# The second feed-forward of a two-layer gated decoder: all experts for all rows, or a dense shared expert and chosen rows in 39 blocks

## The reference, cut to what matters

```python
def _ffn(x, wg, wu, wd):
    return silu(x @ wg.T) * (x @ wu.T) @ wd.T       # 128 -> 344 -> 128
logits = xf @ gate_w.T                              # xf: 2048 x 128, 8 experts
topk_w, topk_idx = top_k(softmax(logits), 2)
topk_w = topk_w / (sum(topk_w) + 1e-20)
cw = zeros((T, 8)).at[arange(T)[:, None], topk_idx].set(topk_w)
y = sum over e of cw[:, e:e + 1] * _ffn(xf, wg[e], wu[e], wd[e])
y = y + _ffn(xf, swg, swu, swd)                     # shared expert
x = x + tanh(g_ffn[1]) * y
```

## Time and profile before

| | us |
|---|---|
| median of 3 runs | 796.5 (796.01 to 798.43) |
| the profiled execution | 796.5 |
| its span, first to last instruction | 794.8 |
| TensorE busy in the span | 658.4 |
| VectorE / ScalarE / GpSimd busy | 610.5 / 397.0 / 395.5 |

### The profile page before, as it was taken

The page is one execution under the profiler, slowest core; times in us unless marked ns, Lnnn a source line. Parts: engine busy times, 40 slices in busy tenths (PEclk is TensorE's granted clock), DMA queues, the critical chain, the costliest instruction groups (busy, mean ns, idle before and its releaser), DMA issues.

```text
span 794.8 us, 13507 instructions
## 1 busy us (share of the span) xinstructions
PE 658.4 (83%) x3446; PEld 499.5 (63%) x3446; DVE 610.5 (77%) x2037; ACT 397.0 (50%) x702; POOL 395.5 (50%) x399
## 2 busy tenths in 40 slices
PE   5653330188999999999999969998799999999995
PEld 2321110176787787877878846665678787877884
DVE  5799999687777777777777785688877777777774
ACT  5533110044565565555565644545456565565653
POOL 4047870036566666665666653000155666656663
PEclk9655555559999999999999975999799999999999
DMA  5424442205877677786776600000146765666761
GB/s 145 78 66 133 137 124 44 47 1 122 153 162 147 139 160 140 147 156 135 158 153 129 134 1 1 2 2 12 37 84 136 161 153 131 159 149 136 160 134 53
DMA packets 73810, 85.90 MB, mean 108 GB/s; under 512 B 39097, under 2 KB 51754, under 8 KB 70760
## 3 DMA queue, kind: packets, MB, share of 16 engines
q1 hardware_dynamic: 66714, 75.05, 44.7%
q0 software_dynamic: 4320, 9.68, 4.1%
q10 hardware_dynamic: 2734, 0.69, 0.4%
HBM read 76.69 MB, written 8.70 MB: 107 GB/s over the span
## 4 chain that ended last, share of the span: by engine, by line
PE 67%; DVE 23%; issue 5%; ACT 2%; DMA 2%; POOL 1%; DVEq 0%; SPq 0%; POOLq 0%; ACTq 0%
PE bank L1034 7%; PE bank L1035 7%; PE bank L1036 7%; PE bank_quad L1190 7%; PE bank_pair L1036 7%; PE bank_pair L1034 7%; PE bank_pair L1035 7%; PE bank_quad L1187 6%; PE bank_quad L1188 6%; DVE arena L1491 3%; PE bank_pair L1083 2%; DVE arena L1487 2%; PE bank L1126 2%; DVE arena L1445 2%; DVE arena L1435 2%
## 5 line engine op out<-in xcount | busy, mean ns | idle before, releaser
L695 POOL TENSOR_TENSOR act_lo<-arena,act_hi 128x512 fp32r<-128x512 f32 x232 | 300.5, 1295 | 193.6 <-ACT act_hi L868 190.8
L1724 DVE TENSOR_TENSOR bank_pair<-arena,bank_pair 128x512 f32<-128x512 f32 x220 | 152.5, 693 | 103.9 <-ACT arena L882 72.9
L882 ACT ACTIVATE arena<-bank 128x512 f32<-128x512 f32 x232 | 139.0, 599 | 185.6 <-PE bank L1036 185.6
L1732 DVE TENSOR_TENSOR arena<-bank_pair,arena 128x512 f32<-128x512 f32 x220 | 152.1, 691 | 16.7 <-DMA arena<-scr_mask 4.5
L868 ACT ACTIVATE act_hi<-arena 128x512 fp32r<-128x512 f32 x232 | 144.6, 623 | 12.8 <-DVE arena L1722 7.1
L1034 PE MATMUL bank_pair<-xn_hi,w_hi 128*128 128x512 f32 x232 | 92.6, 399 | 2.9 <-DVE arena L1722 2.1
L1190 PE MATMUL bank_quad<-act_lo,w_hi 128*128 128x512 f32 x232 | 92.5, 399 | 3.0 <-POOL act_lo L695 3.0
L1034 PE MATMUL bank<-xn_hi,w_hi 128*128 128x512 f32 x232 | 93.8, 404 | 0.1
L1035 PE MATMUL bank<-xn_hi,w_lo 128*128 128x512 f32 x232 | 92.6, 399 | 0.0
L1036 PE MATMUL bank<-xn_lo,w_hi 128*128 128x512 f32 x232 | 92.5, 399 | 0.0
L1036 PE MATMUL bank_pair<-xn_lo,w_hi 128*128 128x512 f32 x232 | 92.3, 398 | 0.0
(11 more groups left out here) (220 smaller groups left out, 1072.6 us busy)
## 6 DMA issues: line engine op xcount, KB each, us to landing
arena<-scr_mask SPq DMA_DIRECT2D x94, 512.0 KB, 6.7
scr_w<-prep_out POOLq DMA_DIRECT2D x25, 192.0 KB, 2.2
w_raw<-scr_w SPq DMA_DIRECT2D x25, 192.0 KB, 6.3
w_raw<-in_L_ffn_expert_gate_k SPq DMA_DIRECT2D x32, 64.0 KB, 5.9
w_raw<-in_L_ffn_expert_up_k SPq DMA_DIRECT2D x32, 64.0 KB, 5.7
w_raw<-in_L_ffn_expert_down_k SPq DMA_DIRECT2D x64, 32.0 KB, 5.2
prep_in<-in_L_ffn_wg POOLq DMA_DIRECT2D x21, 64.0 KB, 2.3
prep_in<-in_L_ffn_wu POOLq DMA_DIRECT2D x21, 64.0 KB, 2.1
```

The lines of the kernel that those rows point to most:

```text
L695: nc.gpsimd.tensor_tensor(act_lo[:, k % 2, :], act_a[:, k % 2, :], act_hi[:, k % 2, :].bitcast(F32), ALU.subtract).then_inc(FF[f]["alo"], 1)
L882: nc.scalar.activation(act_s[:, k % 2, :], ps[4 + k % 2][:], ACT.Silu).then_inc(FF[f]["silu"], 1)
L1724: nc.vector.tensor_tensor(ps[6 + i][:], act_s[:, i, :], ps[6 + i][:], ALU.mult).then_inc(FF[f]["t"], 1)
L1732: nc.vector.tensor_tensor(act_a[:, i, :], ps[6 + i][:], mask[:, j, 512 * k:512 * (k + 1)], ALU.mult).then_inc(FF[f]["act"], 1)
```

## The change

The second feed-forward no longer computes all experts for all rows.

- **Preparation.** The weights are prepared in 27 groups (9 experts x 3 parts of up to 128 hidden numbers) and stored already split: ScalarE copies the high part, TensorE takes it off in PSUM with a matmul by minus one, ScalarE copies the low part; two stores for each group.
- **Dense part** (`dense`). The shared expert alone: 12 units of 9 matmuls. In between, VectorE runs the routing in three parts of 8, 4 and 4 tiles. It also counts, with triangular matmuls (`rows_ahead`), how many earlier rows chose the same expert, which gives each of the 4096 choices its row in a scratch memory with a region for each expert.
- **Send** (`send_rows`). GpSimd writes each tile's rows twice, once for each choice, with 32 indirect DMAs of 128 rows x 528 bytes; a row carries its number and its first expert. `block_table` on VectorE works out which expert and which first row each of 39 blocks of 128 rows has. SyncE then fills up each expert's last block with 8 stores at addresses from a register, and waits for them.
- **Block loop** (`sparse`), 39 blocks written out: SyncE reads a register and loads the block's rows (4 buffers); TensorE turns them, multiplies them by the expert's gate and up weights (which all lie on chip, addressed by a register), 344 columns at a time, turns the activation, and multiplies by the second projection; VectorE sums; GpSimd forms the target row numbers with three small instructions and writes the 128 results with an indirect DMA to a second scratch.
- **Combination** (`add_choices`). SyncE loads both choices' results in row order, VectorE adds them to x by their gate weights.

The core of the diff. SyncE:

```diff
+            sp.wait_ge(s_tab, 3)
+            sp.wait_ge(s_sent, 16 * 2 * TILES)
+            for e in range(E1):
+                n = sp.value_load(table[0:1, 2 * BLOCKS + e:2 * BLOCKS + e + 1], min_val=0, max_val=TOK)
+                sp.dma_start(scr_x[bass.ds(n + e * REGION, BLK), :], pad_rows[:, e, :]).then_inc(s_pad, 16)
+            sp.wait_ge(s_pad, 16 * (SPARE + E1))
+            for k in range(BLOCKS):
+                if k >= XBUF:
+                    sp.wait_ge(s_bt, k - XBUF + 1)
+                    sp.wait_ge(s_row, 3 * (k - XBUF + 1))
+                first = sp.value_load(table[0:1, k:k + 1], min_val=0, max_val=ROWS_X - BLK)
+                sp.dma_start(xb[:, k % XBUF, :], scr_x[bass.ds(first, BLK), :]).then_inc(s_x[k % XBUF], 16)
```

GpSimd:

```diff
+            def send_rows(part):
+
+                pool.wait_ge(s_pos, part + 1)
+                pool.wait_ge(s_xn, (3 * B + ROUTE_BATCH[part]) * ND)
+                pool.wait_ge(s_xnp, (3 * B + ROUTE_BATCH[part]) * (TPB - ND))
+                for t in range(TILES)[ROUTE_TILES[part]]:
+                    for c in range(2):
+                        pool.indirect_dma_start(out=scr_x, out_offset=bass.IndirectOffsetOnAxis(ap=row_of[:, t, c:c + 1], axis=0),
+                                                in_=xrow[:, t, :], in_offset=None).then_inc(s_sent, 16)
...
+            def block_rows_out(k):
+
+                i, j = k % XBUF, k % YBUF
+                pool.wait_ge(s_x[i], 16 * (k // XBUF + 2))
+                if k >= YBUF:
+                    pool.wait_ge(s_ys[j], 16 * (k // YBUF))
+                near, row = y_near[:, j:j + 1], y_row[:, j:j + 1]
+                nc.gpsimd.tensor_scalar(near, xb[:, i, COL_E:COL_E + 1], block_e[:, k:k + 1], float(-TOK),
+                                        ALU.is_equal, ALU.mult).then_inc(s_row, 1)
+                pool.wait_ge(s_row, 3 * k + 1)
+                nc.gpsimd.tensor_tensor(near, near, xb[:, i, COL_TOK:COL_TOK + 1], ALU.add).then_inc(s_row, 1)
+                pool.wait_ge(s_row, 3 * k + 2)
+                nc.gpsimd.tensor_copy(row, near).then_inc(s_row, 1)
+                pool.wait_ge(s_row, 3 * (k + 1))
+                pool.wait_ge(s_byc, k + 1)
+                pool.indirect_dma_start(out=scr_y, out_offset=bass.IndirectOffsetOnAxis(ap=row, axis=0),
+                                        in_=y_b[:, j, :], in_offset=None).then_inc(s_ys[j], 16)
...
+            dense_low(0)
+            normalise(3, B - 1)
+            for u in range(1, POOL_LO):
+                dense_low(u)
+            padding()
+            for part in range(len(ROUTE_TILES)):
+                send_rows(part)
+            pool.wait_ge(s_tab, 3)
+            for k in range(BLOCKS):
+                block_rows_out(k)
```

TensorE:

```diff
+                def turn_rows(k):
+                    pe.wait_ge(s_x[k % XBUF], 16 * (k // XBUF + 2))
+                    if k >= 1:
+                        pe.wait_ge(s_bhi, k)
+                        pe.wait_ge(s_blo, k)
+                    nc.tensor.transpose(ps[4][:, 0:P], xb[:, k % XBUF, 0:H], ident[:]).then_inc(s_bt, 1)
...
+                expert = []
+                for k in range(BLOCKS):
+                    expert.append(pe.value_load(table[0:1, BLOCKS + k:BLOCKS + k + 1], min_val=0, max_val=E1 - 1))
+                    gate_up(k, expert[k])
+                    if k + 1 < BLOCKS:
+                        turn_rows(k + 1)
+                    if k >= 1:
+                        turn_act(k - 1)
+                    if k >= 2:
+                        down(k - 2, expert[k - 2])
+                turn_act(BLOCKS - 1)
+                for k in range(BLOCKS - 2, BLOCKS):
+                    down(k, expert[k])
```

VectorE:

```diff
+                before = {1: [(0, 1), (0, 2), (1, 0)], 2: [(0, 3)], 3: [(0, 4)], 4: [(1, 1), (1, 2)], 5: [(0, 5), (1, 3)],
+                          6: [(1, 4)], 7: [(2, 0), (1, 5)], 8: [(2, 1), (2, 2)], 9: [(2, 3)], 10: [(2, 4)], 11: [(2, 5)]}
...
+                block_low(0)
+                for k in range(BLOCKS):
+                    dve.wait_ge(s_bsilu, k + 1)
+                    dve.wait_ge(s_bgu, 2 * (k + 1))
+                    if k >= 1:
+                        dve.wait_ge(s_bat, k)
+                    nc.vector.tensor_tensor(act_b, gate_b, ps[2 + k % 2][:, 0:I1], ALU.mult).then_inc(s_bact, 1)
+                    if k + 1 < BLOCKS:
+                        block_low(k + 1)
+                    if k >= 1:
+                        act_low(k - 1)
+                    if k >= 2:
+                        block_sum(k - 2)
+                act_low(BLOCKS - 1)
+                block_sum(BLOCKS - 2)
+                block_sum(BLOCKS - 1)
```

More of the change, by code:

```diff
@@ L316, in mask_loaded, with dense_count, raw_loaded @@
+        def dense_count(name, n):
+            return n + (CHUNKS if name in ("yT", "back") else CHUNKS * GROUPS)
+        FF_RAW = [sem(f"ff0_raw_loaded{j}") for j in range(2)]
+        FF_MASK = [sem(f"ff0_mask_loaded{j}") for j in range(2)]
+        RAW_DMAS, MASK_DMAS = 4, 2
+        def raw_loaded(g):
+            return 16 * RAW_DMAS * (g // 2 + 1)
         def mask_loaded(half):
             return 16 * MASK_DMAS * half
-        def products(f, u):
-            return u - CHUNKS * SHARED[f]
@@ L323, in program, with products @@
-        s_x = [sem(f"x_loaded{b}") for b in range(B)]
+        def products(u):
+            return u - CHUNKS * SHARED
+        s_sw = sem("shared_weights_loaded")
+        s_ew = sem("expert_weights_loaded")
+        s_chosen = sem("experts_chosen")
+        s_carry = sem("chosen_carried")
+        s_pre = sem("rows_ahead")
+        s_pos = sem("rows_known")
+        s_sent = sem("rows_sent")
+        s_tab = sem("block_table")
+        s_pad = sem("pads_stored")
+        s_bt = sem("block_rows_turned")
@@ L324, in program @@
+        s_x = [sem(f"x_or_block_loaded{b}") for b in range(B)]
         s_ctx = sem("ctx_loaded")
@@ L348, in program @@
         s_dst = [[sem(f"dist_stored{part}_{b}") for b in range(B)] for part in range(2)]
-        s_dld = [[sem(f"dist_lanes{part}_{b}") for b in range(B)] for part in range(2)]
+        s_dld = [sem(f"dist_lanes{part}") for part in range(2)]
         s_upper = sem("wave_upper")
@@ L423, in load_lanes @@
             engine.dma_start(dl[LANES[b]:LANES[b] + CH, first:last].rearrange("c s w -> c (s w)"),
-                             scr_d[b, :, first:last].rearrange("c s w -> c (s w)")).then_inc(s_dld[part][b], 16)
+                             scr_d[b, :, first:last].rearrange("c s w -> c (s w)")).then_inc(s_dld[part], 16)
         def lanes_laid(engine, part):
-            for b in range(B):
-                engine.wait_ge(s_dld[part][b], 16)
+            engine.wait_ge(s_dld[part], 16 * B)
         def store_path(engine, part, b):
@@ L940, in _ @@
+            for j in range(2):
+                act.wait_ge(s_pst[j], 32 * ((len(PREP) + 1 - j) // 2))
             norm(1)
@@ new lines, in route1 @@
+                    dve.wait_ge(s_chosen, part + 1)
+                    of_part = chosen[:, tiles, :].rearrange("p t e -> p e t")
+                    if part == 0:
+                        nc.vector.tensor_reduce(carry[:, 0, :], of_part, AX_X, ALU.add).then_inc(s_carry, 1)
+                    else:
+                        done(nc.vector.tensor_reduce(chosen_sum[:, part, :], of_part, AX_X, ALU.add))
+                        settle()
+                        dve.wait_ge(s_carry, part)
+                        nc.vector.tensor_tensor(carry[:, part, :], carry[:, part - 1, :], chosen_sum[:, part, :],
+                                                ALU.add).then_inc(s_carry, 1)
@@ L1763, in _ @@
             attention()
-            feed_forward(1)
-            for n in range(CHUNKS):
-                add_ffn(1)(n)
+            dense()
+            sparse()
+            add_choices()
 INPUTS = ["x", "ctx_1024", "g_xattn", "g_ffn", "L0_ffn_router_w", "L0_ffn_shared_gate_w", "L0_ffn_shared_up_w",
```

981 lines of the change are left out of this document (660 added, 321 removed).

## The result

The changed kernel takes 846.2 us (median of 4 runs, 840.9 to 850.2) against 797.5 beside it: a ratio of 1.061, interval 1.053 to 1.069. Two further sets of four runs gave 1.060 (1.058 to 1.062) and 1.061 (1.058 to 1.064). The forecast was 811, so the sign was right and the size was not: +2% was forecast (with a range of 800 to 820), and it is +6%. The profiled execution took 842.4 us, with a span of 839.8.

The account below looks back on a forecast made before the run. TensorE was taken as the bound: busy 83% of the span, never idle in the second feed-forward's loop. First block product at 636.2 + 148.2 for 38 blocks + 6 + 19 = 809.4, and 1.7 outside: 811 us, range 800 to 820.

Parts of the forecast that it names:

- the preparation: Weights of the second feed-forward, prepared early: 26 x 3.7 = 96 us, ending at 145, hidden.
- the sends: 32 indirect DMAs in a row on GpSimd, 586.5 to 618.5, landed at 620.7, later than the block table, so deciding.
- the block loop: 39 blocks bound by a ring through the load buffers: 3.9 us a block, 38 x 3.9 = 148.2 us.
- The fallback: If stores in the preparation cost twice as much to issue: end near 160, path cells some 6 us late; 0 to 6 kept.
- D: GpSimd's time for one indirect DMA: taken as 1.0 us, bounds 0.54 and 1.5.
- The hand-over: From dense part to block loop: pads 9.6 us, landing 2.0, first load 3.0, splitting 0.9; first block product at 636.2.
- V: SyncE's read of a register from the block table: taken as 0.7 us, bounds 0.05 and 1.7.
- The clock: TensorE's clock in the block loop: a mixture of full and half, granted between 0.5 and 0.8.
- The tail: After the last product: sum, store, 2 MB of rows back, last eight small sums, output store; 19 us against 9 before.
- Cheap ring: Rival for sends and block loop: D = 0.6, V = 0.3, full clock, 3.4 us a block, 775 us; chance 0.30.
- dear issue: Rival for sends and block loop: D = 1.4, V = 1.3, 4.5 us a block, 853 us; chance 0.12.
- T: Time of one block in the block loop: taken as 3.9 us; at 3.5 the stage would fall under its former 235.

Follow-up runs that it names:

- Experiment 1: Changed kernel with its weight preparation pipelined: two PSUM banks in turn, loads issued before the stores of the group two back; 830.6 us, ratio 1.041.
- run 4: Changed kernel with all 32 indirect sends held back until the block table is ready; 857.5 us, ratio 1.075.
- experiment 6: Changed kernel with three pauses in the sends and the eight pads stored ahead of SyncE's wait for the sends; 832.6 us, ratio 1.044.
- experiment 2: Changed kernel with GpSimd working out the next block's row numbers before it issues the current block's scatter; 799.0 us, ratio 1.002.
- run 14: Changed kernel with twelve one-column copies more on VectorE ahead of the dense part; 841.4 us in one run.

## Why the prediction was wrong

Two steps made 22 of the 30 us that the forecast of the span was off, the preparation and the sends. The mechanism of the block loop, the largest term, was right. The account, from the forecast's span of 809.4 to 839.8:

| step of the prediction | forecast | measured | off |
|---|---|---|---|
| start of the dense part | 560.0 | 569.7 | +9.7 |
| from there to the first send | 26.5 | 29.4 | +2.9 |
| first send to last landing | 34.2 | 46.3 | +12.1 |
| pads, first load, to the first block product | 15.5 | 14.1 | -1.4 |
| 38 blocks | 148.2 | 151.6 | +3.4 |
| last block and tail | 25 | 28.8 | +3.8 |

- **The preparation is the step that failed in its conclusion.** "That is 26 x 3.7 = 96, so 145: hidden" was wrong: 26 x 4.35 = 113, so 163. Before the change a group took 2.95 us, from the stores at 49.0 and 119.7, where the forecast's cycle gives 2.75; the change added 1.40 and not 0.85. The sum of a group left out that both stores had become dearer (0.76 against 0.57), and that one PSUM bank and the order of the stores put landing, turning, two copies and the correcting product in one row. The fallback was named (end near 160, 6 us late, "I keep 0 to 6") but priced at half: at the first feed-forward it cost 12.2, of which attention gave 2.5 back. Experiment 1 takes it back whole. The forecast had named this among its signs of being wrong: a preparation that ends behind 155 us.
- **The sends are the step that was mis-sized.** D was 1.0 and the instruction takes 0.96, but "32 indirect DMAs, one behind the other" at 1.0 leaves out 0.30 from one to the next; plain DMAs follow at their own length. 31 x 0.27 is 8 us of the 12; run 4 shows that it is no matter of what runs beside it. Another 4.5 are GpSimd's wait for the last row numbers through the stall, which no step had; the last landing came some 0.9 sooner than put.
- **The hand-over** was right in size. A pad takes 1.10 us where V + 0.5 = 1.2 was put. With the issue of 0.33 taken off, 0.77 is left for V, but only 0.27 to 0.28 of it is the read itself (646.77 in the chain above; 0.48 for the first); the rest is work on the value and on the address. The Trainium skill (DMA: Bandwidth & Descriptors, section Latency and other measured facts) has a floor of about 600 ns for a tensor_load: the reads of this trace lie below it. That the pads need not wait for the sends at all was not seen; it is worth 9 us (experiment 6).
- **The block loop was right**, in its size (3.99 against 3.9) and in its mechanism: the chain runs through just the members named, and experiment 2, which spreads this ring alone over one block more, took 46 us out. The clock was a mixture as forecast, at 0.83 a little above the 0.5 to 0.8 that was named.
- **The tail** was 22.8 us from the last product at 817 and not 19. The last scatter starts at 820.9 and has landed at 823.2, 6.2 us behind the last product where 3.9 was put: its row numbers stand behind the scatter before it, the ring once more. The first rows landed 4.4 us later and the last at 833.5, 10.3 us later (8.5 forecast). What decided was that the 32 small sums stand in one row behind the first landing, 9.4 us, and not only the last eight (2.5) behind the last:

```profile
827.69 2.31 DVE L2252 SCALAR_TENSOR_TENSOR x_res<-arena,x_res 128x128 f32<-128x128 f32 x8 [9.98 <-DMA arena<-scr_y]
830.29 6.76 DVE L2252 SCALAR_TENSOR_TENSOR x_res<-arena,x_res 128x128 f32<-128x128 f32 x24 [0.29 <-DMA arena<-scr_y]
```

- **A slip outside the sum.** "TensorE loses 160 us of work" doesn't follow from the forecast's own terms: 209 less 35 for the dense part and less 39 x 2.3 = 90 for the blocks is 84. Its busy time fell by 29 (658.4 to 629.7), in which products at the half clock count longer.
- **The rivals.** Cheap ring and dear issue were both wrong in D and V. Of the cheap case it held that a shorter loop can turn the sign, but not at the T = 3.5 that it gives for the forecast hand-over: with the hand-over as it was, T = 2.78 only broke even (run 2), and the versions that win have both a T of 2.8 or less and the first turn at 637 or before.

## What to carry to other kernels

When a change replaces work by a chain of latencies, the work that is left out is no measure of the gain; follow each ring once round, and look first for an instruction that stands in its queue behind a wait that it does not need (here three tiny ones on GpSimd, for 46 us, and eight stores on SyncE, for 9). A preparation called hidden has to be priced with its waits and compared with the moment when its engine is next wanted, however far that is from the change. Count for a repeated instruction the distance to its next, not its length alone. Where the profile names no releaser for a long wait, look up the instruction that makes the awaited value: if its record ended long before, suspect a late signal.

## What the runs showed of the hardware

- An indirect DMA that sends 128 rows of 528 bytes takes GpSimd 0.96 us, and 0.30 more pass before the next starts, with or without other work beside it (runs 4 and the first): 1.27 from one to the next. One of 128 rows of 512 bytes takes 1.07 to 1.08, and a small operation of GpSimd followed 0.08 later.
- A plain store of the same 192 KB in 384 pieces takes GpSimd 0.76 us where 0.55 to 0.57 was measured for 128 pieces.
- A read of a register from the table by SyncE takes 0.26 to 0.28 us, 0.48 for the first of the row; with the work on value and address a register-addressed store follows the one before it at 1.10 us.
- VectorE, ScalarE and behind them TensorE can stand for 20 to 33 us in all beside unbroken indirect sends, on some occasions and not on others, for the same kernel and on the same chip. TensorE's signals are then on record up to 24 us behind their products, and 0.01 to 0.02 us otherwise. A wait of 1.4 to 1.9 us for the landing let the engines on each time it was seen. Why the signals are late is open.
- The loop bound by the ring ran at a granted clock of 0.83 with TensorE busy for 116 of 160 us, and at 0.88 with 111 of 157 in run 14; that of run 2 at 0.96 with 90 of 105.
